# Work beside moved ahead of the second maximum, a reciprocal moved behind it, and one sequence's tokens turned in the first layers

## The chip, the core and the metric

The kernel runs on one core of a Trainium2 chip. Its engines each run their own queue in order: TensorE (PE in the profile; PEld is its loading of weights), VectorE (DVE), ScalarE (ACT), GpSimd (POOL) and SyncE (SP, which here only starts transfers). They wait for each other by semaphores. The metric is the device time of one execution in microseconds.

## The reference, cut to what is computed

Two sequences of 2048 tokens with 256 channels go through four layers, each with a layer norm in front and a residual around it.

```python
x = x + ssm(layernorm(x))         # state scan over the tokens, gelu, layer norm, nan_to_num
x = x + mixer(layernorm(x))       # sigmoid(xr Wr) * (relu(xk Wk)^2 Wv), xr and xk mix a token with the one before
x = x + attention(layernorm(x))   # 16 heads of 64, keys and values from a latent of 128, causal softmax
x = x + mixer(layernorm(x))
```

## The kernel before, in words

**Memory and banks.** X holds all tokens, 32 tiles of 128. There are 8 banks for products: 0 to 3 are `scores`, 4 `heads_out`, 5 and 6 `two_heads`, 7 `beside`.

**Order.** The class `Plan` writes one list of tasks, and each engine's program walks through that list and issues its part of each task. So the order of tasks is the order on every engine, and an engine whose part of a task waits holds up all of its parts of later tasks. `add` appends a task; `need` appends it with what it depends on, unless it is done.

**First layers** (`first_layers`, rounds k = 0 to 11). In round k the scan runs on block k (512 tokens), the tail of the first layer on block k-1, the first mixer's `turn`, `mix_tokens`, `products` and `square` on block k-2, and its `update` on block k-3. Blocks 0 to 3 are sequence 0. Behind round 7 the statistics of sequence 0 for the attention are complete (`inverse_std seq 0`, version 2). From round 8 on less and less work is left.

**Attention** (`attention`). All engines but SyncE's later part first wait until the last `update` is done (`attention_start`). For each pair of tiles `att_normal` (ScalarE, two normalisations `att_xn`), `turn_tiles` (TensorE transposes, a copy `att_xT_hi` on ScalarE, the rest `att_xT_lo` on VectorE) and for each block `latent` make the inputs. A unit is one sequence, one pair of heads and one block of 512 queries (j = 0 to 3); four units are a cycle, and there are 16 cycles. For a unit: `query`, `key` and `value` products; `maximum` (L755: two heads' scores into `two_heads`, and VectorE's reduction into `part_max`, L985, or L982 where the mask applies), whose next matmuls need the reduction before; `turn_max`; then steps over 128 keys each: `score` (L778 to L784), exponentials on ScalarE (L1194), sums on GpSimd (L1276), and `weigh` (L796, `heads_out`). At the end `denominators`, `invert` (the reciprocal L1010 and two small transfers by SyncE), `scale_out`, `two_parts` and `project`.

**The loop of steps** takes two steps at a time: a maximum of a later unit; the two scores; a second maximum; a filler; the two `weigh` of the pair before; a third maximum; other work. A filler is the open task with the earliest due time among query, key, value, latent, turn_tiles, turn_max and project; all write bank 7. A pair of steps is called diagonal where the causal mask cuts it (`scores<-scores,limit` on VectorE, L995): the last two pairs of each unit. In the first of them the scores have 512 and 384 columns, in the second 256 and 128. `query`, `key` and `project` have a part on VectorE (`q_lo`, `k_lo`, the sum into X), `value` and `turn_max` have none.

```python
            if at < goal:
                maximum()
            due("invert")
            for step in steps[s:s + 2]:
                self.need("score", *step)
            if at < goal:
                maximum()
            else:
                chore()
            filler(10 ** 6)
```

Of the kernel before, what the change touches and what calls it, by code (L numbers as in the profile page):

```python
# [5 lines left out]
ALU = mybir.AluOpType  # L6
ACT = mybir.ActivationFunctionType
# [5 lines left out]
P = 128  # L13
# [19 lines left out]
NDEN, QUAD = 8, 32  # L33
DVE_OUT = 62
# [22 lines left out]
class Plan:  # L57
# [104 lines left out]
    def first_layers(self):  # L162
# [15 lines left out]
        for k in range(NBL + 4):  # L178
# [38 lines left out]
            if k - 4 == NBLK - 1:  # L217
                self.add("inverse_std", "seq", 0, 0, NT, 2)

# [101 lines left out]
    def attention(self):  # L321
        self.freed = [None] * 8
        self.add("attention_start")
        self.need("turn_tiles", 0, 0)
        self.add("latent_weights")
# [57 lines left out]
        for s in range(0, len(steps) + 2, 2):  # L383
# [16 lines left out]
            filler(10 ** 6)  # L400
# [30 lines left out]
def build(nc, u, wA, wF, wKD, wPair, aDiag, h0, gb, mu, out):  # L431
# [4 lines left out]
    with ExitStack() as ctx:  # L436
# [26 lines left out]
        def empty(task, i=0):  # L463
# [11 lines left out]
        minus_mean_ok, zeros_ok, soft_v, soft_a, decay_ok = (  # L475
            sem(s) for s in ("minus_mean_ok", "zeros_ok", "soft_v", "soft_a", "decay_ok"))
# [25 lines left out]
        def channel_memory(where, w):  # L502
            return {"xn": sb(where, f"xnF{w}", [P, 2, TPB, C]), "xT": sb(where, f"xTF{w}", [P, 2, CH, BLK + 1]),
                    "mix": sb(where, f"mix{w}", [P, 2, 2, CH, BLK]), "relu": sb(where, f"relu{w}", [P, CH, BLK]),
                    "kact": sb(where, f"kact{w}", [P, 2, CH, BLK]),
                    "gate": sb(where, f"gate{w}", [P, 2, TPB, C])}

        M = {}
        with ExitStack() as tail_scope:
            gamma_beta = sb(tail_scope, "gamma_beta", [P, 2, C])  # L510
            G = sb(tail_scope, "G", [P, NB * NT, C])
            nrm = sb(tail_scope, "nrm", [P, 2, 2, C])
            clp = sb(tail_scope, "clp", [P, 2, 2, C])
            msk = sb(tail_scope, "msk", [P, 2, 2, C])
# [7 lines left out]
            zeros = sb(tail_scope, "zeros", [P, BLK])  # L522
            decay = sb(tail_scope, "decay", [P, CH, BLK])
# [5 lines left out]
        with ExitStack() as ph:  # L529
            axT_hi = sb(ph, "att_xT_hi", [P, CH, T], F32R)  # L530
            axT_lo = sb(ph, "att_xT_lo", [P, CH, T], F32R)
            lat_hi = sb(ph, "lat_hi", [P, T], F32R)
            lat_lo = sb(ph, "lat_lo", [P, T], F32R)
            axn = [sb(ph, f"att_xn{i}", [P, C]) for i in range(4)]
# [3 lines left out]
            wP_raw = sb(ph, "wP_raw", [P, WPC])  # L538
            kd_hi = sb(ph, "kd_hi", [P, CH, RANK], F32R)
            kd_lo = sb(ph, "kd_lo", [P, CH, RANK], F32R)  # L540
# [9 lines left out]
            kd_raw = prob[NPROB - 1][:, 0, 0:CH * RANK].rearrange("p (c r) -> p c r", c=CH)  # L550
# [831 lines left out]
```

## Time and profile before

| | |
|---|---|
| median of 3 runs | 2247.73 us (2247.59 to 2248.44) |
| profiled execution: its time, its span | 2246.04 us, 2244.7 us |
| TensorE busy | 2060.4 us (92%) |
| VectorE, ScalarE, GpSimd busy | 1331.9, 1102.8, 1426.5 us |
| TensorE busy in 0 to 56 us | 28.31 us, granted clock 0.97 |
| in 56 to 112, 112 to 168, 168 to 224 us | 51.08, 52.70, 47.56 us, clock 0.94, 0.97, 0.94 |
| in 224 to 280, 280 to 336 us | 35.07, 36.39 us, clock 0.76, 0.63 |
| in 800 to 900, 900 to 1000 us | 96.69, 96.07 us, clock 1.00, 0.98 |

### The profile page before, as it was taken

The page shows a single profiled execution, that of the slowest core. Times are in us where ns is not written, and L with a number is a line of the kernel's source. Part 1 is how long each engine was busy: PE and PEld are TensorE (multiplying, and loading weights), DVE is VectorE, ACT ScalarE, POOL GpSimd, SP SyncE. Part 2 cuts the span into 40 slices and gives each one's busy share as a digit, 9 for nine tenths or more (in the row PEclk, how much of TensorE's full clock was granted, in tenths as well). Part 3 has the DMA queues.
Part 4 walks back from the last instruction along what each step waited for, and adds up shares of the span by engine and source line. Part 5 has one row for each costly group of instructions (what it writes and reads, how often), then busy time and mean ns, then how long its engine had stood idle before and what let it go on. Part 6 is the DMA issues. An engine that isn't in the chain of part 4 may idle for free.

```text
span 2244.7 us, 35674 instructions
## 1 busy us (share of the span) xinstructions
PE 2060.4 (92%) x13104; PEld 1269.9 (57%) x13104; DVE 1331.9 (59%) x2713; ACT 1102.8 (49%) x2226; POOL 1426.5 (64%) x812
## 2 busy tenths in 40 slices
PE   5998669999999999999989999999999999999989
PEld 3666345555555555555555555555555555555556
DVE  5888446575656565656565656566656565656353
ACT  4775534444444444444454444444444444444575
POOL 0333305776777777777757677777777777777832
PEclk9999769999999999999999999999999999999999
DMA  3000000000000000000000000000000000000001
GB/s 108 1 1 1 10 7 6 10 18 10 18 11 18 11 18 11 18 11 18 10 18 11 13 11 19 9 22 6 19 9 23 11 18 11 18 11 11 25 24 57
DMA packets 25788, 37.03 MB, mean 16 GB/s; under 512 B 6544, under 2 KB 14864, under 8 KB 25616
## 3 DMA queue, kind: packets, MB, share of 16 engines
q1 hardware_dynamic: 25616, 34.76, 5.0%
q8 instruction: 106, 1.74, 0.3%
q14 instruction: 66, 0.54, 0.1%
HBM read 30.02 MB, written 4.46 MB: 15 GB/s over the span
## 4 chain that ended last, share of the span: by engine, by line
PE 65%; DVE 19%; ACT 6%; issue 5%; POOL 4%; DMA 0%; ACTq 0%; DVEq 0%; POOLq 0%
PE heads_out L796 18%; PE beside L615 14%; PE two_heads L755 8%; PE scores L778 4%; PE scores L784 4%; PE scores L782 4%; PE scores L780 4%; DVE part_max L985 4%; PE scores L615 2%; POOL acc L1276 2%; ACT prob L1194 2%; DVE stats L835 2%; PE beside L807 2%; PE beside L763 1%; PE two_heads L615 1%
## 5 line engine op out<-in xcount | busy, mean ns | idle before, releaser
L1276 POOL TENSOR_TENSOR acc<-acc,prob 128x1024 f32<-128x1024 f32 (+3 forms) x512 | 1017.1, 1987 | 228.5 <-ACT prob L1194 172.7
L1194 ACT ACTIVATE prob<-scores 128x512 f32<-128x512 f32 (+3 forms) x1280 | 579.4, 538 | 636.4 <-DVE scores L995 327.8
L985 DVE TENSOR_REDUCE part_max<-two_heads 128x2 f32<-128x1024 f32 x384 | 468.7, 1221 | 309.1 <-PE two_heads L755 308.8
L796 PE MATMUL heads_out<-prob,V 128*64 128x512 f32 (+3 forms) x2560 | 549.1, 550 | 0.0
L755 PE MATMUL two_heads<-k_hi,q_hi 64*128 64x512 f32 (+3 forms) x1280 | 278.9, 431 | 70.2 <-DVE part_max L982 36.5
L982 DVE CUSTOM_DVE_ANT_0 two_heads<-two_heads,mask 128x128 f32<-128x128 f32 (+3 forms) x512 | 241.8, 514 | 119.2 <-PE two_heads L755 119.1
L796 PEld LDWEIGHTS heads_out<-prob,V 128*64 128x64 f32 x2560 | 157.8, 138 | 232.1 <-issue 210.4
L755 PEld LDWEIGHTS two_heads<-k_hi,q_hi 64*128 64x128 f32 x1280 | 121.3, 186 | 239.3 <-issue 102.4
L778 PE MATMUL scores<-q_hi,k_hi 64*128 64x512 f32 (+3 forms) x1280 | 236.9, 364 | 1.0 <-ACT neg_max L1181 0.8
L784 PE MATMUL scores<-neg_max,sel 64*128 64x512 f32 (+3 forms) x1280 | 236.9, 363 | 0.0
L782 PE MATMUL scores<-q_lo,k_hi 64*128 64x512 f32 (+3 forms) x1280 | 236.3, 363 | 0.0
L780 PE MATMUL scores<-q_hi,k_lo 64*128 64x512 f32 (+3 forms) x1280 | 235.7, 362 | 0.0
L1271 POOL TENSOR_TENSOR acc<-prob 128x768 f32<-128x768 f32 (+1 forms) x64 | 144.0, 2250 | 139.7 <-ACT prob L1194 139.3
L1285 POOL TENSOR_TENSOR oT_lo<-oT,oT_hi 128x512 fp32r<-128x512 f32 x62 | 79.3, 1279 | 177.6 <-ACT oT_hi L1211 177.6
L1029 DVE TENSOR_TENSOR X<-X,beside 128x512 f32<-128x512 f32 x126 | 86.0, 683 | 91.3 <-PE beside L615 90.9
L782 PEld LDWEIGHTS scores<-q_lo,k_hi 64*128 64x128 f32 x1280 | 122.5, 185 | 19.0
L784 PEld LDWEIGHTS scores<-neg_max,sel 64*128 64x128 f32 x1280 | 122.6, 185 | 18.4
L780 PEld LDWEIGHTS scores<-q_hi,k_lo 64*128 64x128 f32 x1280 | 122.4, 186 | 18.7
L778 PEld LDWEIGHTS scores<-q_hi,k_hi 64*128 64x128 f32 x1280 | 122.4, 186 | 16.7 <-issue 5.0
L995 DVE TENSOR_TENSOR scores<-scores,limit 128x256 f32<-128x256 f32 x256 | 103.0, 430 | 21.5 <-PE scores L784 21.2
L968 DVE SCALAR_TENSOR_TENSOR q_lo<-beside,q_hi 128x512 fp32r<-128x512 f32 x62 | 42.9, 692 | 97.2 <-ACT q_hi L1163 97.2
L615 PE MATMUL beside<-wP_hi,oT_hi 128*128 128x256 f32 x252 | 84.6, 336 | 13.2 <-DVE X L1029 7.5
(298 smaller groups left out, 3011.4 us busy)
## 6 DMA issues: line engine op xcount, KB each, us to landing
rden<-rden_rows SPq DMA_DIRECT2D x128, 128.0 KB, 2.9
wP_raw<-wPair SPq DMA_DIRECT2D x16, 384.0 KB, 3.2
X<-u SPq DMA_DIRECT2D x8, 512.0 KB, 8.7
out<-X SPq DMA_DIRECT2D x8, 512.0 KB, 2.9
den<-den_rows SPq DMA_DIRECT2D x64, 4.0 KB
rden_rows<-inverse SPq DMA_DIRECT2D x64, 4.0 KB, 1.4
wA_sb<-wA SPq DMA_DIRECT2D x1, 768.0 KB, 6.8
wFa<-wF SPq DMA_DIRECT2D x1, 768.0 KB, 7.7
```

Source lines behind the costliest of these rows:

```text
L615: made = pe.matmul(dst, l, r, start=first and n == 0, stop=last and n == len(pairs) - 1)
L755: made = pe.matmul(two_heads[:, h, 0:width], q[head(h), t * P:(t + 1) * P], k[head(h), 0:width], start=True, stop=True)
L778: pe.matmul(bank(task, h)[:, x0:], k_hi[g][head(h), kc], q_hi[i][head(h), x0:], start=True, stop=False)
L780: pe.matmul(bank(task, h)[:, x0:], k_lo[g][head(h), kc], q_hi[i][head(h), x0:], start=False, stop=False)
L782: pe.matmul(bank(task, h)[:, x0:], k_hi[g][head(h), kc], q_lo[i][head(h), x0:], start=False, stop=False)
L784: pe.matmul(bank(task, h)[:, x0:], sel[head(h), :], neg_max[i][head(h), x0:], start=False, stop=True).then_inc(full(task, h)[0], 1)
L796: made = pe.matmul(heads_out[head(h), x0:], V[(idx - j + c) % NVS][:, tt, head(h)], prob[step % NPROB][:, h, x0:], start=t == 0, stop=t == ...
L982: made = ve.tensor_tensor_reduce(out=two_heads[:, h, 0:width], in0=two_heads[:, h, 0:width], in1=mask[:, BLK - width:], scale=1.0, scalar= ...
L985: made = ve.reduce_max(part_max[:, t, :, c:c + 1], two_heads[:, :, 0:width], AX.X)
L1194: ac.activation(prob[step % NPROB][:, h, x0:], bank(task, h)[:, x0:], ACT.Exp).then_inc(empty(task, h)[0], 1)
L1271: po.tensor_tensor(total[:, :, x0:], old[:, :, x0:], new[:, :, x0:], ALU.add).then_inc(acc_ok, 1)
L1276: po.tensor_tensor(total[:, :, x0:], total[:, :, x0:], new[:, :, x0:], ALU.add).then_inc(acc_ok, 1)
```

## The change

It has three parts. In the loop of steps, a pair that has a diagonal step takes its filler ahead of the second maximum, and `invert` is issued behind that maximum in every pair. In the first layers, the split of the latent's weights, all eight `turn_tiles` and the four `latent` of sequence 0 are issued in rounds 8, 9 and 10 (with NBL = 8), ahead of `attention_start`. The third part makes room: the tiles of the attention that are now written early get memory of their own (a scope `early` that closes behind the attention), and the first layers use less. `G` is a ring of three blocks, `msk` one buffer, `relu` is written into `kact` and squared in place, and the scan's factor `decay` is one column that is read repeated, for which `zeros` and the filling of `decay` go. The weights of the first pair of heads are loaded as soon as the latent's weights are split.

```diff
@@ first_layers
             if k - 4 == NBLK - 1:
                 self.add("inverse_std", "seq", 0, 0, NT, 2)
+                self.add("latent_weights")
+                self.need("att_normal", 0, 0)
+            if k == NBL:
+                for t in range(0, NT // 2, 2):
+                    self.need("turn_tiles", 0, t)
+            if k == NBL + 1:
+                for t in range(NT // 2, NT, 2):
+                    self.need("turn_tiles", 0, t)
+                self.need("latent", 0, 0)
+                self.need("latent", 0, 1)
+            if k == NBL + 2:
+                self.need("latent", 0, 2)
+                self.need("latent", 0, 3)
@@ attention
-        self.freed = [None] * 8
         self.add("attention_start")
-        self.need("turn_tiles", 0, 0)
-        self.add("latent_weights")
@@
         for n in range(TPB):
             maximum()
-            if n == 0:
-                self.need("turn_tiles", 0, TPB)
-            if n == 1:
-                self.need("latent", 0, 1)
@@
             if at < goal:
                 maximum()
-            due("invert")
             for step in steps[s:s + 2]:
                 self.need("score", *step)
+            diagonal = any(t >= TPB * UNITS[idx][2] for idx, t in steps[s:s + 2])
+            if diagonal:
+                filler(10 ** 6)
             if at < goal:
                 maximum()
             else:
                 chore()
-            filler(10 ** 6)
+            due("invert")
+            if not diagonal:
+                filler(10 ** 6)
@@ vector_program, ssm_setup and ssm_states
-                    ve.memset(zeros[:, :], 0.0).then_inc(zeros_ok, 1)
-                    for h in range(CH):
-                        ve.tensor_scalar(decay[:, h, :], zeros[:, :], a_col[:, h:h + 1], None, ALU.subtract).then_inc(decay_ok, 1)
+                    ve.tensor_scalar(decay[:, :], a_col[:, :], -1.0, None, ALU.mult).then_inc(decay_ok, 1)
-                        ve.tensor_tensor_scan(xs[:, s_, m, :], decay[:, m, :], bank(task, m), init, ALU.mult, ALU.add).then_inc(empty(task, m)[0], 1)
+                        ve.tensor_tensor_scan(xs[:, s_, m, :], decay[:, m:m + 1].broadcast_to([P, BLK]), bank(task, m), init, ALU.mult, ALU.add).then_inc(empty(task, m)[0], 1)
@@ scalar_program, ssm_output and products
+                        g = k % (NG * TPB)
+                        if i >= NG:
+                            w.wait_ge(normalised, plan.normal["tail_norm", k - NG * TPB] + 2)
-                        ac.activation(M[f]["relu"][:, m, :], bank(task, m), ACT.Relu).then_inc(empty(task, m)[0], 1)
+                        ac.activation(M[f]["kact"][:, i % 2, m, :], bank(task, m), ACT.Relu).then_inc(empty(task, m)[0], 1)
@@ sync_program
+            sp.dma_start(kd_raw[:, :, :], wKD).then_inc(kd_in, 16)
-                if kind == "attention_start":
-                    w.wait_ge(ffn["a"]["x_plus_ffn"], 2 * NBL)
-                    sp.dma_start(kd_raw[:, :, :], wKD).then_inc(kd_in, 16)
+                if kind == "latent_weights":
+                    w.wait_ge(kd_ok, 1)
                     sp.dma_start(wP_raw[:, :], wPair[0]).then_inc(wP_in, 16)
```

The order of instructions on VectorE at the first diagonal pair of a block 0, before (the `ISA` rows with 128x256 are the reduction of the second maximum, those with 128x384 that of the third):

```order
L995 TENSOR_TENSOR scores<-scores,limit 128x2x128 x2
L982 ISA two_heads,part_max<-two_heads,mask 128x256
L982 ISA part_max 128x1
L982 ISA two_heads,part_max<-two_heads,mask 128x256
L982 ISA part_max 128x1
L968 SCALAR_TENSOR_TENSOR q_lo<-beside,q_hi 128x512
L982 ISA two_heads,part_max<-two_heads,mask 128x384
```

and with the change:

```order
L1004 TENSOR_TENSOR scores<-scores,limit 128x2x128 x2
L977 SCALAR_TENSOR_TENSOR q_lo<-beside,q_hi 128x512
L991 ISA two_heads,part_max<-two_heads,mask 128x256
L991 ISA part_max 128x1
L991 ISA two_heads,part_max<-two_heads,mask 128x256
L991 ISA part_max 128x1
L991 ISA two_heads,part_max<-two_heads,mask 128x384
```

`q_lo` moved from behind the second maximum's reduction to ahead of it; on TensorE the six matmuls of `query` moved ahead of that maximum's.

VectorE again, in a pair of steps of block 1 that isn't diagonal, before (the reciprocal is `invert`, the two `wP_lo` a split of weights):

```order
L950 TENSOR_TENSOR wP_lo<-wP_raw,wP_hi 128x256
L1010 RECIPROCAL inverse<-den 16x64
L985 TENSOR_REDUCE part_max<-two_heads 128x2
L950 TENSOR_TENSOR wP_lo<-wP_raw,wP_hi 128x256
L973 TENSOR_TENSOR k_lo<-beside,k_hi 128x512
```

and with the change:

```order
L959 TENSOR_TENSOR wP_lo<-wP_raw,wP_hi 128x256
L994 TENSOR_REDUCE part_max<-two_heads 128x2
L959 TENSOR_TENSOR wP_lo<-wP_raw,wP_hi 128x256
L1019 RECIPROCAL inverse<-den 16x64
L982 TENSOR_TENSOR k_lo<-beside,k_hi 128x512
```

The reciprocal moved past the reduction and the second split, to just ahead of `k_lo`.

ScalarE in the first layers, behind round 8 (the square root `std` ends that round's statistics, `xnFa` is the normalisation of the last block for the mixer), before:

```order
L1119 ACTIVATE kacta<-relua 128x512 x2
L1042 ACT_TABLE_LOAD
L1042 ACTIVATE std<-std 128x4
L1035 ACTIVATE xnFa<-X,minus_mean,rstd 128x256 x4
L1090 ACTIVATE xTFa<-scores 128x512 x2
```

and with the change:

```order
L1130 ACTIVATE kacta<-kacta 128x512 x2
L1051 ACT_TABLE_LOAD
L1051 ACTIVATE std<-std 128x4
L1161 ACTIVATE att_xT_hi<-scores 128x2x256
L1044 ACTIVATE att_xn<-X,minus_mean,rstd 128x256 x2
L1161 ACTIVATE att_xT_hi<-scores 128x2x256
L1044 ACTIVATE att_xn<-X,minus_mean,rstd 128x256 x2
L1161 ACTIVATE att_xT_hi<-beside 128x2x256
L1044 ACTIVATE att_xn<-X,minus_mean,rstd 128x256 x2
L1161 ACTIVATE att_xT_hi<-scores 128x2x256
L1044 ACTIVATE att_xn<-X,minus_mean,rstd 128x256 x2
L1044 ACTIVATE xnFa<-X,minus_mean,rstd 128x256 x4
```

Four copies and four pairs of normalisations of the attention now stand ahead of the last block's normalisation. On TensorE the transposes between them stand ahead of the update of block 6.

## Rows read from the trace of the kernel before

**Rows 1.** The page's busy times: engine, us, share of the span, instructions

```profile
PE 2060.4 (92%) x13104; PEld 1269.9 (57%) x13104; DVE 1331.9 (59%) x2713; ACT 1102.8 (49%) x2226; POOL 1426.5 (64%) x812
```

**Rows 2.** TensorE's waits, 400 to 2110 us: us in total, times, longest

```profile
PE two_heads L755 <- DVE part_max L982: 30.6, 37, 1.8
```

**Rows 3.** Timeline, second diagonal pair of a block 2: start, us, instruction, idle before

```profile
965.62 0.69 DVE L973 TENSOR_TENSOR k_lo<-beside,k_hi 128x512 fp32r<-128x512 f32 x1 [3.10 <-ACT k_hi L1169]
...
967.42 0.50 PE L755 MATMUL two_heads<-k_hi,q_hi 64*128 64x512 f32 x2 [1.21 <-DVE part_max L982]
...
969.33 3.16 PE L796 MATMUL heads_out<-prob,V 128*64 128x512 f32 x8
```

**Rows 4.** Timeline of TensorE: the same place in other cycles

```profile
634.31 0.49 PE L755 MATMUL two_heads<-k_hi,q_hi 64*128 64x512 f32 x2 [1.21 <-DVE part_max L982]
...
747.48 0.50 PE L755 MATMUL two_heads<-k_hi,q_hi 64*128 64x512 f32 x2 [1.21 <-DVE part_max L982]
...
857.45 0.50 PE L755 MATMUL two_heads<-k_hi,q_hi 64*128 64x512 f32 x2 [1.21 <-DVE part_max L982]
...
1079.02 0.50 PE L755 MATMUL two_heads<-k_hi,q_hi 64*128 64x512 f32 x2 [1.21 <-DVE part_max L982]
...
1990.90 0.49 PE L755 MATMUL two_heads<-k_hi,q_hi 64*128 64x512 f32 x2 [1.21 <-DVE part_max L982]
```

**Rows 5.** Stretch: us, PE, PEld, DVE, ACT, POOL busy, granted clock, DMA share, GB/s

```profile
969.30:971.00 1.70, 1.70 (x6) 0.45 (x7) 0.24 (x3) 1.11 (x2) 0.37 (x1) 0.55 0.05 10
```

**Rows 6.** Timeline at the first diagonal pair of a block 0

```profile
907.37 1.85 ACT L1194 ACTIVATE prob<-scores 128x512 f32<-128x512 f32 x4 [2.68 <-DVE scores L995]
...
907.80 0.42 DVE L982 CUSTOM_DVE_ANT_0 two_heads<-two_heads,mask 128x256 f32<-128x256 f32 x1
...
908.52 0.14 DVE L982 DVE_READ_ACCUMULATOR2_ANT part_max<- 128x1 f32 x1
...
909.74 0.69 DVE L968 SCALAR_TENSOR_TENSOR q_lo<-beside,q_hi 128x512 fp32r<-128x512 f32 x1 [1.08 <-ACT q_hi L1163]
909.75 0.44 PE L755 MATMUL two_heads<-k_hi,q_hi 64*128 64x384 f32 x2
...
910.35 0.56 DVE L982 CUSTOM_DVE_ANT_0 two_heads<-two_heads,mask 128x384 f32<-128x384 f32 x1
...
911.53 0.51 PE L755 MATMUL two_heads<-k_hi,q_hi 64*128 64x512 f32 x2 [0.48 <-DVE part_max L982]
```

**Rows 7.** Timeline around a reciprocal in a pair that isn't diagonal

```profile
920.54 0.53 DVE L1010 RECIPROCAL inverse<-den 16x64 f32<-16x64 f32 x1
...
921.00 1.15 DVE L985 TENSOR_REDUCE part_max<-two_heads 128x2 f32<-128x1024 f32 x1
...
923.43 0.68 DVE L973 TENSOR_TENSOR k_lo<-beside,k_hi 128x512 fp32r<-128x512 f32 x1
...
924.16 0.64 PE L807 MATMUL beside<-acc,ones 128*32 128x256 f32 x8 [0.69 <-DVE k_lo L973]
```

**Rows 8.** Timeline of the start and of the hand-over to the attention

```profile
15.33 0.88 DVE L882 TENSOR_SCALAR decay<-zeros,a_col 128x512 f32<-128x512 f32 x2
...
271.68 1.09 ACT L1035 ACTIVATE att_xn<-X,minus_mean,rstd 128x256 f32<-128x256 f32 x2 [5.88 <-POOL X L1240]
...
273.83 0.60 ACT L1150 ACTIVATE att_xT_hi<-scores 128x512 fp32r<-128x512 f32 x1 [1.06 <-PE scores L702]
...
276.60 0.60 ACT L1150 ACTIVATE att_xT_hi<-scores 128x512 fp32r<-128x512 f32 x1 [1.20 <-PE scores L702]
...
283.00 0.80 PE L615 MATMUL scores<-lat_hi,wP_hi 128*128 128x512 f32 x1 [2.08 <-DVE wP_lo L950]
...
305.02 0.42 PE L778 MATMUL scores<-q_hi,k_hi 64*128 64x512 f32 x2
...
331.10 0.45 PE L778 MATMUL scores<-q_hi,k_hi 64*128 64x256 f32 x2
```

**Rows 9.** Chain of waits: the first latent (start, us, what)

```profile
278.02 2.91 PE beside L615 x6
```

More of the change, by code:

```diff
@@ L503, in channel_memory @@
             return {"xn": sb(where, f"xnF{w}", [P, 2, TPB, C]), "xT": sb(where, f"xTF{w}", [P, 2, CH, BLK + 1]),
-                    "mix": sb(where, f"mix{w}", [P, 2, 2, CH, BLK]), "relu": sb(where, f"relu{w}", [P, CH, BLK]),
-                    "kact": sb(where, f"kact{w}", [P, 2, CH, BLK]),
+                    "mix": sb(where, f"mix{w}", [P, 2, 2, CH, BLK]), "kact": sb(where, f"kact{w}", [P, 2, CH, BLK]),
                     "gate": sb(where, f"gate{w}", [P, 2, TPB, C])}
         M = {}
+        early = ctx.enter_context(ExitStack())
+        axT_hi = sb(early, "att_xT_hi", [P, CH, T], F32R)
+        axT_lo = sb(early, "att_xT_lo", [P, CH, T], F32R)
+        lat_hi = sb(early, "lat_hi", [P, T], F32R)
+        lat_lo = sb(early, "lat_lo", [P, T], F32R)
+        axn = [sb(early, f"att_xn{i}", [P, C]) for i in range(4)]
+        kd_hi = sb(early, "kd_hi", [P, CH, RANK], F32R)
+        kd_lo = sb(early, "kd_lo", [P, CH, RANK], F32R)
+        wP_raw = sb(early, "wP_raw", [P, WPC])
+        kd_raw = wP_raw[:, 0:CH * RANK].rearrange("p (c r) -> p c r", c=CH)
         with ExitStack() as tail_scope:
             gamma_beta = sb(tail_scope, "gamma_beta", [P, 2, C])
-            G = sb(tail_scope, "G", [P, NB * NT, C])
+            G = sb(tail_scope, "G", [P, NG * TPB, C])
             nrm = sb(tail_scope, "nrm", [P, 2, 2, C])
             clp = sb(tail_scope, "clp", [P, 2, 2, C])
-            msk = sb(tail_scope, "msk", [P, 2, 2, C])
+            msk = sb(tail_scope, "msk", [P, 2, C])
             fin = sb(tail_scope, "fin", [P, 2, 2, C], mybir.dt.uint32)
@@ L521, in build @@
             a_col = sb(tail_scope, "a_col", [P, CH])
-            zeros = sb(tail_scope, "zeros", [P, BLK])
-            decay = sb(tail_scope, "decay", [P, CH, BLK])
+            decay = sb(tail_scope, "decay", [P, CH])
             state0 = sb(tail_scope, "state0", [P, CH])
@@ L561, in build @@
             oT_lo = sb(ph, "oT_lo", [P, BLK], F32R)
+        early.close()
         with ExitStack() as ph:
@@ L1114, in scalar_program @@
                     _, f, i = task
-                    if i >= 2:
-                        w.wait_ge(*full(("update", f, i - 2), 1))
                     for m in range(CH):
                         w.wait_ge(*empty(("products", f, i), m))
-                        ac.activation(M[f]["kact"][:, i % 2, m, :], M[f]["relu"][:, m, :], ACT.Square).then_inc(ffn[f]["kact"], 1)
+                        ac.activation(M[f]["kact"][:, i % 2, m, :], M[f]["kact"][:, i % 2, m, :], ACT.Square).then_inc(ffn[f]["kact"], 1)
                 elif kind == "attention_start":
```

30 lines of the change are left out of this document (11 added, 19 removed).

## Prediction, written before the changed kernel was run

> **What bounds the kernel now.** I read the busy row of the page first. TensorE is busy for 2060.4 of 2244.7 us, 92%, and every other engine 64% or less [rows 1]. So TensorE's idle time is what a change of order can win or lose, about 184 us. The stretches in the table ahead put 85 us of it before 336 us, in the first layers and the start of the attention; in the long middle TensorE is 96 to 97% busy. There the list of waits shows one wait that matters to this change: the `two_heads` matmuls of a maximum wait for VectorE to have read the maximum before, 30.6 us in 37 waits on L982 alone [rows 2]. Then I read three places of one cycle (four units of one pair of heads, about 110 us, sixteen of them) in the order of time, and last the hand-over from the first layers to the attention.
>
> **Part 1: the filler ahead of the second maximum, where it wins.** In the diagonal pairs the filler now stands before the maximum. It can only fill a wait where there is a filler, and where TensorE waits. Both hold at the second diagonal pair of block 2, where the filler is `value`: TensorE waits 1.21 us there, and starts the four `heads_out` products behind the value product at 969.33 [rows 3]. This wait stands in nearly every cycle, thirteen times between 519 and 1991 us (twice 1.76 us), of which six stand here [rows 3, 4]. With `value` in front, TensorE can start it when bank 7 is free, that is when `k_lo` ends at 966.31 (965.62 + 0.69), instead of sitting until 967.42. The value product lasts 1.48 us whichever way, so about 1.0 us of the 1.21 is won and 0.3 us of waiting for the bank is left. VectorE has nothing to do for `value`, so nothing gets in front of the second reduction. 14 places x 1.0 = **-14 us**. The waits in the other second pairs, like the 0.48 us at 911.53 [rows 6], have no filler behind them and stay.
>
> **The clock there.** Behind the wait at 967.42 the granted clock is 0.55 in the next 1.70 us [rows 5], near the lower of the two levels (1.2 GHz). Five of the thirteen places are followed by such a stretch. The price is in the distance between equal places: 109.97 us from 747.48 to 857.45 and the same on to 967.42, but 111.60 from 967.42 to 1079.02 and 113.17 from 634.31 to 747.48 [rows 3, 4]. So a drop costs 1.6 us, or 3.2 where it lasts longer; all five together some 11 us. If the wait is gone, I expect them gone.
>
> **Part 2: where it loses.** At the first diagonal pair of block 0 the filler is `query`, and `query` has a part on VectorE, `q_lo`, which now stands ahead of the second maximum's reduction. `q_lo` cannot be early: it waits for `q_hi` on ScalarE, which comes behind the four exponentials of 907.37 (1.85 us), whatever TensorE does. So it starts at 909.74 as now [rows 6]. The reduction of the second maximum, which ran in 907.80 to 908.66 and so 0.86 us, then starts where the next one starts now, 910.35, and ends at 911.21. TensorE follows 0.05 us behind such an end (911.48 to 911.53), so the next maximum starts at 911.26 instead of 909.75: a **new wait of 1.5 us**. Behind it on TensorE are the next score pair and everything else; its cover is only the short `heads_out` products of the block that ends (256 and 128 columns, 0.8 us). The wait at 911.53 comes 1.78 us behind 909.75 and moves along, so nothing is won back. 15 places x 1.5 = **+22.5 us**. The fillers `project`, `turn_max` and `value` in the other first pairs are free: there 1.7 us of `heads_out` products stand between the second maximum and the next, more than a reduction of 1.2 us, and no wait is there now to fill.
>
> **Part 3: the reciprocal behind the second maximum.** It takes 0.53 us on VectorE and now often runs while VectorE would wait. Ahead of `k_lo` at 923.43 the chain on VectorE is full: the reduction at 921.00 began 0.4 us late because of the reciprocal at 920.54. Moved behind, it lets the reduction start at about 920.75 and holds `k_lo` up by 0.3 us; TensorE waits for that `k_lo` already, 0.69 us at 924.16 [rows 7]. In two more places of a cycle it lands in front of a bank's reading for which TensorE comes almost at once, some 0.15 us each. That is 0.6 us x 15 = **+9 us**, between 0 (the chain has slack) and 0.8 x 16 = 13. The transfers that it starts come 2 to 3 us later; GpSimd would wait for them about as long once a cycle, and is idle for longer than that before its next reading of ScalarE's copy. I cost it at nothing; if the slack is not there, up to 1 us a cycle.
>
> **Part 4: sequence 0's tokens in the first layers.** The cost first. A pair of tiles (two normalisations, four transposes, a copy, a subtraction) is a closed circle of ScalarE and TensorE: 2.77 us from copy to copy (273.83 to 276.60) [rows 8]. In the last-but-one round four such pairs now stand on ScalarE ahead of the last block's normalisation: three circles and the rest of one, 9.9 us, on the path. One normalisation more (1.09 us) stands ahead in the round before. In the last round three circles stand between the squares and the last block's update on TensorE, 8.2 us, and two latents, 2.91 us each at the lower clock [rows 9]. Sum: 24.9 us, which moves the first key product from 283.00 to about 298, because the 11.3 us from 271.68 to it fall to about 1.6 us (only the weights' split is left). That is +15. Now the gain. From key to first score, 22.0 us now (283.00 to 305.02), two pairs and a latent go: about -5. From there to the second score pair, 26.1 us (to 331.10), two pairs, a latent and the wait behind it go: -7.4. The last two pairs and latent, and their waits, go from the next 30 us: -3. So this is about level when the clock stays as low as now (0.63 in 280 to 336 us, by the table ahead), and -9 us if TensorE, busier before the last products, gets its full clock back sooner. I take **-3**, with -10 and +7 as ends.
>
> **Small terms.** `decay` and `zeros` leave the start: the two operations of 0.88 us at 15.33 stand right before the statistics on which all waits [rows 8]; **-0.7**. The scan reads its factor as one column repeated; no row shows that form, and I take the same 1.26 us, 0.3 us more or less for each of sixteen. `relu` into `kact`, one `msk`, the ring `G`: each new wait is for something done long before.
>
> **Sum.** Waits: -14 + 22.5 + 9 - 3 - 0.7 = +13.8. Clock: the five drops go (-11), but the new place is idle for 1.5 and then 0.48 us within 3.3 us, more than at the old one. I let half of the fifteen drop at 1.6 us, +12, and set both to nothing. The profiled execution took 2246.04 us, 1.7 us under the median of 2247.73; its time with the sum is 2259.8, and counted from the median, as a run would be compared, it is 2261.5: I forecast **2261 us**.
>
> On the clock the Trainium skill (TensorE: Matmul & The Clock Gate, A second HAM failure mode: psum-queue depth-cycling) tells of a kernel whose TensorE idles briefly between groups of matmuls often enough for the clock to go back and forth, so that throughput suffers more than by the idle time. By that, the new place should drop in most cycles; the trace has it in five of thirteen at the old one.
>
> **Rivals.** (a) *The clock gains and nothing is paid for it*: the drops at `value` go, `query` brings none. For it: eight of the thirteen waits at `value` brought none. 2261 - 12 = 2249 us, no change. (b) *Faster*: the same, and TensorE also holds its full clock from the last update on, so that part 4 gives its -9 or -10. It decides whether the last block's products of 512 columns, now at half rate for their first 4 us, run at full rate. 2249 - 7 = 2242, and 2238 if half of part 3 is slack. (c) *The clock falls at `query` in nearly every cycle*, some of them for the longer 3.2 us: 13 x 1.6 to 2 more than nothing, less the half I counted: 2261 + 12 = 2273, up to 2282. (d) *The change doesn't do it*: the order shows `q_lo` ahead of the reduction in fifteen places and `value` ahead in thirteen, so this is out.
>
> **Chances.** Forecast (2252 to 2266) 0.42; (c) and worse 0.20; (a) 0.23; (b) 0.15. A measurement of this kernel can tell about 0.2% (4.5 us) from no change. Slower by more than that 0.60, within it 0.25, faster 0.15. The range 2242 to 2282 leaves out the far ends of (b) and (c).
>
> **What would show it.** In the profile after: a wait of about 1.5 us of `two_heads` for `part_max` behind each `q_lo` of block 0, with `q_lo` ahead of a 256-column reduction; no wait over 0.4 us before `value`; 0.9 to 1.0 us instead of 0.69 before the denominators; the cycle longer by 1 us where no drop falls; first key product at 293 to 300 us and second score pair at 325 to 335. Wrong it would be if the wait at `query` is under 0.5 us, or if the attention's first step starts past 320 us.

## The result, and the profile after

The changed kernel takes 2251.64 us in the median of ten runs, the kernel before 2246.31 us in ten runs beside them: a ratio of 1.0027, with a 95% interval of 1.0017 to 1.0036. It is slower by some 5 to 6 us, the way that was forecast, and inside the range; but the forecast said +14, more than twice as much. The profiled execution has a span of 2249.3 us, 4.6 more than before (2244.7).

The busy row of the page, and the waits of TensorE in 400 to 2110 us (us in total, times, longest), of the changed kernel:

```profile
PE 2058.6 (92%) x13104; PEld 1263.7 (56%) x13104; DVE 1344.5 (60%) x2711; ACT 1100.2 (49%) x2226; POOL 1424.4 (63%) x812
...
PE two_heads L767 <- DVE part_max L991: 26.1, 34, 1.3
PE two_heads L767 <- DVE part_max L994: 19.9, 37, 1.6
PE beside L819 <- DVE k_lo L982: 15.3, 14, 1.1
...
PE beside L627 <- DVE k_lo L982: 2.9, 14, 0.6
```

Against [rows 2], the masked maxima (now L991) cost 26.1 us and not 30.6: much of one wait went and much of another came. The denominators' wait for `k_lo` went from 10.0 to 15.3 us in fourteen places. The last row is what is left at `value`.

**One cycle without a clock drop.** The denominators' product stands once in every unit and serves as a mark. Four stretches between five marks make a cycle. The timeline rows of these marks (start, duration, instruction, the wait before it), first of before, then of after:

```profile
803.66 0.64 PE L807 MATMUL beside<-acc,ones 128*32 128x256 f32 x8
814.20 0.64 PE L807 MATMUL beside<-acc,ones 128*32 128x256 f32 x8 [0.69 <-DVE k_lo L973]
835.18 0.64 PE L807 MATMUL beside<-acc,ones 128*32 128x256 f32 x8
872.40 0.64 PE L807 MATMUL beside<-acc,ones 128*32 128x256 f32 x8
913.62 0.64 PE L807 MATMUL beside<-acc,ones 128*32 128x256 f32 x8
```

```profile
796.15 0.64 PE L819 MATMUL beside<-acc,ones 128*32 128x256 f32 x8
807.09 0.64 PE L819 MATMUL beside<-acc,ones 128*32 128x256 f32 x8 [1.10 <-DVE k_lo L982]
828.11 0.64 PE L819 MATMUL beside<-acc,ones 128*32 128x256 f32 x8
864.36 0.64 PE L819 MATMUL beside<-acc,ones 128*32 128x256 f32 x8
907.16 0.64 PE L819 MATMUL beside<-acc,ones 128*32 128x256 f32 x8
```

The four differences are 10.54, 20.98, 37.22 and 41.22 us before, and 10.94, 21.02, 36.25 and 42.80 after. I call the stretches K (the wait for `k_lo` is in it), N, V (the place of `value` in block 2) and Q (the place of `query`). K is longer by 0.40, N by 0.04, V shorter by 0.97, Q longer by 1.58: +1.05 us a cycle.

**The place of `query`.** TensorE and VectorE of the changed kernel, where [rows 6] stood before:

```profile
901.30 0.87 PE L808 MATMUL heads_out<-prob,V 128*64 128x256 f32 x8
901.86 0.69 DVE L977 SCALAR_TENSOR_TENSOR q_lo<-beside,q_hi 128x512 fp32r<-128x512 f32 x1 [1.83 <-ACT q_hi L1174]
902.47 0.42 DVE L991 CUSTOM_DVE_ANT_0 two_heads<-two_heads,mask 128x256 f32<-128x256 f32 x1
...
903.19 0.14 DVE L991 DVE_READ_ACCUMULATOR2_ANT part_max<- 128x1 f32 x1
903.39 0.44 PE L767 MATMUL two_heads<-k_hi,q_hi 64*128 64x384 f32 x2 [1.22 <-DVE part_max L991]
...
905.07 0.51 PE L767 MATMUL two_heads<-k_hi,q_hi 64*128 64x512 f32 x2 [0.37 <-DVE part_max L991]
```

VectorE waits 1.83 us for ScalarE before `q_lo`, reduces the 256-column maximum only behind it, and the next maximum's matmuls wait 1.22 us. The wait after that one is 0.37 instead of 0.48 us.

**The place of `value`**, where the 1.21 us of [rows 3] stood. A wait of 0.18 us is left, and the maximum behind the product has none:

```profile
960.40 0.33 PE L627 MATMUL beside<-wP_hi,lat_hi 128*128 128x128 f32 x1 [0.18 <-DVE k_lo L982]
...
961.89 0.50 PE L767 MATMUL two_heads<-k_hi,q_hi 64*128 64x512 f32 x2
```

**The hand-over**, where [rows 8] gave 283.00, 305.02 and 331.10: first key product, first score, second score pair.

```profile
294.94 0.47 PE L627 MATMUL beside<-lat_hi,wP_hi 128*128 128x512 f32 x1 [2.17 <-DVE wP_lo L959]
...
311.23 0.42 PE L790 MATMUL scores<-q_hi,k_hi 64*128 64x512 f32 x2
...
329.43 0.41 PE L790 MATMUL scores<-q_hi,k_hi 64*128 64x256 f32 x2
```

The first denominators' product starts at 349.81 us and not at 353.39: 3.6 us earlier.

**The clock.** A stretch-by-stretch view with slices of 3 us (PE, PEld, DVE, ACT, POOL busy, granted clock, DMA share, GB/s) around a `query` place at which the clock fell, behind the waits of 1.22 and 0.37 us at 1709.79 and 1711.47:

```profile
1707.00:1710.00 3.00, 1.78 (x14) 0.89 (x15) 1.47 (x5) 1.83 (x4) 2.13 (x2) 1.00 0.00 0
1710.00:1713.00 3.00, 2.63 (x24) 1.64 (x24) 2.73 (x9) 1.00 (x4) 0.41 (x2) 0.81 0.00 0
1713.00:1716.00 3.00, 3.00 (x18) 0.76 (x16) 0.59 (x3) 0.14 (x1) 1.60 (x2) 0.62 0.00 0
```

What the lower level takes, the loss, is (1 - granted clock) times 3 us, summed over such slices: here 0.57 + 1.14 = 1.7 us. Between 336 and 2110 us every drop in every trace of this study comes to 1.7 us or twice that, except where 2110 us cuts one. In sum it is 17.0 us before (five drops at `value` places, 11.9 us, and three others, one of them behind a wait for ScalarE's `att_xn` between the two sequences) and 12.0 us after (five at `query` places, 8.5 us, and two others; none at `value`).

So a span splits in two: this loss, and the rest. Before it is 2227.7 + 17.0, after 2237.3 + 12.0: **+9.6 us of rest, and 5.0 us that the clock gives back.** The rest isn't all at full clock. In 0 to 336 us, where TensorE is often idle, the same sum is 44.4 us before and 39.2 after. A cleaner measure of the waits in the loop is the time from the first to the 63rd of the marks less the loss in it: 1740.4 us before and 1753.5 after, **+13.1 us**. The first mark is 3.6 us earlier, and that makes the +9.6 within 0.1 us. The experiments ask which part does what, and whether the parts add up.

### The profile page after: what moved, and what is told of

Read it like the earlier page. It is cut to its first block, busy times and chain, and to the rows that moved or that the text cites. A ratio compares the mean times of both kernels' runs of the same rounds, so it can differ in the third digit from the quotient of the medians.

```text
span 2249.3 us, 35656 instructions
## 1 busy us (share of the span) xinstructions
PE 2058.6 (92%) x13104; PEld 1263.7 (56%) x13104; DVE 1344.5 (60%) x2711; ACT 1100.2 (49%) x2226; POOL 1424.4 (63%) x812
## 4 chain that ended last, share of the span: by engine, by line
PE 69%; DVE 17%; ACT 7%; issue 5%; POOL 2%; DMA 0%; ACTq 0%; DVEq 0%; SPq 0%; POOLq 0%
PE heads_out L808 19%; PE beside L627 14%; PE two_heads L767 9%; PE scores L790 5%; PE scores L796 5%; PE scores L794 5%; PE scores L792 4%; PE scores L627 3%; DVE part_max L994 3%; ACT prob L1205 2%; PE beside L819 2%; DVE stats L847 2%; DVE X L1038 2%; PE beside L775 1%; DVE two_heads L991 1%
## 5 line engine op out<-in xcount | busy, mean ns | idle before, releaser
L991 DVE CUSTOM_DVE_ANT_0 two_heads<-two_heads,mask 128x128 f32<-128x128 f32 (+3 forms) x512 | 242.0, 514 | 147.3 <-PE two_heads L767 147.1
L1292 POOL TENSOR_TENSOR oT<-oT,rden 128x512 f32<-128x512 f32 x62 | 79.2, 1278 | 128.3 <-DMA rden<-rden_rows 106.1
L790 PEld LDWEIGHTS scores<-q_hi,k_hi 64*128 64x128 f32 x1280 | 121.8, 186 | 15.8 <-issue 4.0
```

The source lines that it names most:

```text
L790: pe.matmul(bank(task, h)[:, x0:], k_hi[g][head(h), kc], q_hi[i][head(h), x0:], start=True, stop=False)
L991: made = ve.tensor_tensor_reduce(out=two_heads[:, h, 0:width], in0=two_heads[:, h, 0:width], in1=mask[:, BLK - width:], scale=1.0, scalar= ...
```

## The experiments

The table has the medians of all kernels, the ratio to the kernel before with its 95% interval, the profile's span split as above, and the four stretches of a cycle without a drop. Each kernel is compared with the kernel before as timed beside it.

| kernel | median us | ratio to before (95%) | span = rest + loss in 336 to 2110 us | K, N, V, Q |
|---|---|---|---|---|
| before | 2246.3 to 2247.8 | 1 | 2244.7 = 2227.7 + 17.0 | 10.54, 20.98, 37.22, 41.22 |
| changed | 2251.64 | 1.0027 (1.0017 to 1.0036) | 2249.3 = 2237.3 + 12.0 | 10.94, 21.02, 36.25, 42.80 |
| a1_invert_alone | 2255.22 | 1.0032 (1.0020 to 1.0045) | 2254.6 = 2232.4 + 22.2 | 10.94, 20.83, 37.3, 41.2 |
| a2_query_alone | 2287.37 | 1.0186 (1.0159 to 1.0212) | 2291.9 = 2247.5 + 44.4 | 10.53, 20.96, 37.3, 42.6 |
| a3_others_alone | 2223.95 | 0.9899 (0.9883 to 0.9916) | 2222.7 = 2217.6 + 5.1 | 10.53, 21.15, 36.2, 41.4 |
| a4_front_alone | 2245.34 | 1.0001 (0.9987 to 1.0016) | 2246.5 = 2222.6 + 23.9 | 10.53, 20.97, 37.3, 41.2 |
| b1_q_lo_behind | 2231.80 | 0.9932 (0.9920 to 0.9945) | 2231.6 = 2223.0 + 8.6 | 10.94, 21.02, 36.2, 41.76 |
| b2_all_but_query | 2219.49 | 0.9877 (0.9862 to 0.9892) | 2220.3 = 2213.5 + 6.8 | 10.53, 21.17, 36.2, 41.4 |
| b3_value_ahead | 2221.30 | 0.9892 (0.9875 to 0.9909) | 2218.1 = 2207.3 + 10.8 | 10.53, 20.96, 36.2, 41.2 |
| b5_value_invert_last | 2231.56 | 0.9932 (0.9919 to 0.9944) | 2228.9 = 2217.0 + 11.9 | 10.53, 20.84 then 21.8, 36.2, 41.2 |
| c1_value_alone | 2220.59 | 0.9892 (0.9871 to 0.9912) | 2219.8 = 2211.3 + 8.5 | 10.53, 20.95, 36.2, 41.2 |
| c2_value_and_query | 2244.52 | 1.0014 (0.9996 to 1.0032) | 2242.9 = 2229.2 + 13.7 | 10.54, 20.95, 36.2, 42.6 |
| c3_front_again | 2247.62 | 1.0024 (1.0004 to 1.0044) | 2254.5 = 2223.8 + 30.7 | 10.54, 20.94, 37.3, 41.2 |
| c4_value_held | 2206.33 | 0.9835 (0.9809 to 0.9861) | 2205.6 = 2197.1 + 8.5 | 10.53, 20.28, 36.2, 41.2 |

The second table keeps the start apart from the loop, and looks at more than one execution. Every execution has its granted clock on record, to three digits; (1 - granted clock) x span is its loss over the whole length. The last two columns are means over all executions of a kernel, good to about 1 us (the kernel before has a rest of 2180.1 and a loss of 65.0 us, to which the changed kernel is compared; the others are compared with the executions beside them).

| kernel | first mark, us | marks 1 to 63 less their loss, against before | all executions: rest, against before | loss, against before |
|---|---|---|---|---|
| before | 353.39 | 0 | 0 | 0 |
| changed | 349.81 | +13.1 | +15.8 | -10.5 |
| a1_invert_alone | 352.99 | +3.4 | +3.3 | +4.1 |
| a2_query_alone | 353.05 | +18.4 | +19.4 | +23.1 |
| a3_others_alone | 354.35 | -9.4 | -7.0 | -15.6 |
| a4_front_alone | 348.85 | -0.4 | -1.2 | +1.2 |
| b1_q_lo_behind | 348.12 | -2.2 | -0.3 | -15.0 |
| b2_all_but_query | 346.98 | -10.6 | -11.6 | -15.5 |
| b3_value_ahead | 349.45 | -14.3 | -13.4 | -11.0 |
| b5_value_invert_last | 347.97 | -6.3 | -5.2 | -10.1 |
| c1_value_alone | 351.37 | -14.3 | -13.2 | -12.0 |
| c2_value_and_query | 348.98 | +6.0 | +7.9 | -5.1 |
| c3_front_again | 350.86 | -1.5 | +0.5 | +5.1 |
| c4_value_held | 350.25 | -24.1 | -23.3 | -14.7 |

The rows before, a1, a2, c1 and c2 have moved nothing ahead of the first mark, and still it comes between 348.98 and 353.39 us. So a start that is some us earlier in one trace says little.

### The reciprocal alone (a1_invert_alone)

```diff
             if at < goal:
                 maximum()
-            due("invert")
             for step in steps[s:s + 2]:
                 self.need("score", *step)
             if at < goal:
                 maximum()
             else:
                 chore()
+            due("invert")
             filler(10 ** 6)
```

> The kernel before with one part of the change alone: the reciprocal stands behind the second maximum, in all pairs. The waits' theory, from the trace of the changed kernel: the denominators' wait for k_lo grows from 0.69 to 1.10 us, and the next stretch by 0.04, once a cycle, so +0.44 x 15 = +6.6 us, about 1.003 of before. The rival, that the reciprocal costs nothing and the two maxima before k_lo are late because of the other edits: within 1 us of before, and the wait stays at 0.69.

The wait for `k_lo` of this kernel (waits of TensorE, 400 to 2110 us):

```profile
PE beside L807 <- DVE k_lo L973: 15.6, 14, 1.4
```

K grows from 10.54 to 10.94, as expected; but N falls from 20.98 to 20.83, so a cycle costs 0.25 to 0.28 us. Between the marks that is 3.4 us, half of what was expected. The medians say 7.6 us; the rest is clock, 5.2 us more loss in this trace and 4.1 in the mean of its executions.

### The query alone (a2_query_alone), and the clock that its shift costs elsewhere

```diff
+            if diagonal and coming() == "query":
+                filler(10 ** 6)
+                diagonal = None
             if at < goal:
                 maximum()
             else:
                 chore()
-            filler(10 ** 6)
+            if diagonal is not None:
+                filler(10 ** 6)
```

(`coming()` gives the kind of the filler that would be taken; `diagonal` is as in the change.)

> The kernel before with the filler ahead of the second maximum of a diagonal pair only where the filler is query (fifteen places). The waits' theory: each such stretch of a cycle is longer by 1.2 us of waits and 0.2 to 0.4 us of the changed order on TensorE, together 1.4 to 1.6, so +21 to +24 us. The clock theory adds to this: the new place is followed by a stretch at the lower clock in some seven cycles, 1.6 us or more each, while the five drops at value stay, so +33 to +39 us (1.015 to 1.017). The rival, that the clock falls about equally often whatever the order is: +21 to +24 us (1.010).

It lost 40 us, just above the 33 to 39 us of the upper theory. The waits of TensorE in 400 to 2140 us, and the two slices around the `value` place at 862.33, where the wait was 1.22 us, as before:

```profile
PE two_heads L764 <- DVE part_max L991: 46.7, 52, 1.8
...
861.00:864.00 3.00, 1.78 (x12) 1.43 (x11) 3.00 (x10) 1.00 (x4) 1.08 (x1) 0.88 0.00 0
864.00:867.00 3.00, 3.00 (x12) 1.65 (x13) 0.44 (x3) 1.11 (x2) 0.66 (x1) 0.50 0.00 0
```

Between the marks, without the loss, it costs 18.4 us, Q being longer by 1.4. Some 27 us of this trace are clock (23 in the mean of its six executions), and they do not lie at `query` alone, where the clock fell in seven of fifteen places: at the untouched `value` places the clock fell in ten of thirteen cycles, where it had fallen in five, and often for twice as long (V of 40.4 us instead of 37.3 or 38.9).

### The other fillers alone (a3_others_alone)

The same edit with `coming() != "query"`.

> The kernel before with the filler ahead only where it is value, turn_max or project; query and the reciprocal stay where they were. The waits' theory: -0.96 us at each of thirteen places of value in block 2, nothing or up to +0.2 us at each of the 43 others (a change of the matmuls' form on TensorE that costs a little), so -12 to -5 us. With the clock theory, the drops that follow the wait at value go too, another -11 to -15 us: -16 to -27 us (0.988 to 0.993). The rival, that the clock falls about equally often whatever the order: -5 to -12 us (0.995 to 0.998).

24 us faster than before, as the clock theory had it. V is 36.2 us in all the regular cycles. But Q and N are longer by 0.17 each: `project`, `turn_max` and `value` of block 1, ahead where TensorE had nothing to wait for, cost that.

### Sequence 0 in the first layers alone (a4_front_alone, c3_front_again)

The changed kernel with the loop's lines as they were before. The second kernel is the first again, the same program.

> The changed kernel with the loop of the kernel before: only the tokens of sequence 0 in the first layers and the changed memory are left. From the trace of the changed kernel: the first denominators' product starts at 349.81 instead of 353.39 us, so -3.6 us, and nothing after it: -3 to -4.5 us (0.998 to 0.9987). The rival, that the buffers' new places or the other parity of the banks cost something in the loop, so that what the whole change lost beyond the waits comes from here: 0 to +6 us.

> The changed kernel with the loop of before once more, to narrow its interval: sequence 0's tokens in the first layers, and the memory, alone. If the 4.5 us by which the loop starts earlier come through: 0.998 to 0.999 of before. If the clock drops that its trace showed at the first block, between the sequences and at the end (1.4, 3.4 and 1.4 us more than before) come in most runs, they take it back: 0.9995 to 1.001.

The first mark comes at 348.85 and 350.86 us, in the mean 2.3 us earlier than in the five kernels with the old first layers named above, whose own spread is larger. In the times nothing arrives: the medians are 2.3 below and 0.6 above before, and the ratio of c3_front_again, 1.0024, lies above both ranges that were expected. Nor is there a clear gain without the clock: over all executions the rest is 1.2 us below and 0.5 above before.

The lower clock was moved about. The last stretch of the hand-over, first of before, then of the changed kernel (a4 and c3 too have less loss there):

```profile
309.00:336.00 27.00, 15.75 (x57) 9.49 (x57) 12.88 (x28) 6.27 (x14) 4.16 (x4) 0.56 0.00 0
```

```profile
309.00:336.00 27.00, 17.49 (x85) 10.62 (x84) 16.18 (x32) 7.10 (x15) 4.14 (x4) 0.75 0.05 15
```

The loss is 12.0 us before and 6.8 after. Behind it, the slices of a4_front_alone at the first units, and the same of before:

```profile
342.00:345.00 3.00, 3.00 (x16) 2.36 (x16) 1.55 (x2) 0.88 (x2) 0.00 (x0) 0.50 0.00 0
...
360.00:363.00 3.00, 3.00 (x12) 1.00 (x10) 1.09 (x1) 1.30 (x5) 1.99 (x2) 0.58 0.03 7
```

```profile
342.00:345.00 3.00, 2.60 (x22) 1.43 (x18) 1.94 (x3) 2.82 (x6) 1.10 (x1) 1.00 0.00 0
...
360.00:363.00 3.00, 2.40 (x23) 1.68 (x21) 2.79 (x7) 0.60 (x1) 1.79 (x1) 1.00 0.00 0
```

Two drops stand there that before does not have, 3.4 us, and both traces show them. The two traces of this one program have spans of 2246.5 and 2254.5 us, 8 us apart, of which 6.8 are loss at the lower clock: so far did the clock alone move one execution.

### The q_lo put back behind the reduction (b1_q_lo_behind)

The changed kernel, edited in VectorE's program alone:

```diff
+            behind = list(tasks)
+            for n in range(1, len(behind) - 1):
+                if [behind[n + i][0] for i in (-1, 0, 1)] == ["score", "query", "maximum"]:
+                    behind[n], behind[n + 1] = behind[n + 1], behind[n]
-            for task in tasks:
+            for task in behind:
```

> The changed kernel with one thing undone: on VectorE alone q_lo stands behind the second maximum's reduction again, at the sixteen places where query stands ahead of the second maximum; TensorE and ScalarE keep the changed order. The theory that q_lo ahead of the reduction makes the new wait: the wait of 1.22 us goes to 0, the stretch of a cycle with it falls from 42.79 to about 41.4 us, and with it the seven drops of the clock behind it, so 15 x 1.3 = 20 us and some 10 to 15 us of clock below the changed kernel: 2216 to 2232 us. The rival, that TensorE's own order (the maximum's products behind those of query) makes the wait: it stays over 0.8 us and the time within 5 us of 2252.

```profile
896.77 0.45 PE L767 MATMUL two_heads<-k_hi,q_hi 64*128 64x384 f32 x2 [0.17 <-DVE part_max L995]
898.45 0.50 PE L767 MATMUL two_heads<-k_hi,q_hi 64*128 64x512 f32 x2 [0.37 <-DVE part_max L995]
```

The wait is 0.17 us instead of 1.22 with TensorE's order unchanged, Q falls from 42.80 to 41.76, no drop stands at `query` any more, and the kernel is 20 us faster than the changed one, at the slow end of what was expected (a wait of 0 and a Q of 41.4 us). So `q_lo` ahead of the reduction made the wait. That is shown. What is left of `query` ahead, Q of 41.76 against 41.40 in b2_all_but_query, is the price of TensorE's own order: the wait of 0.17 us and 0.2 us without a wait.

### Leaving query behind, and which fillers pay (b2_all_but_query, b3_value_ahead)

> The changed kernel with query behind the second maximum and the reciprocal where it was before; value, turn_max and project stay ahead, and the first layers as in the change. If the parts add up: 2224 from the kernel with the others ahead, less 0 to 3 us for the first layers, 2220 to 2225 us (0.988 to 0.990 of before). If the first layers' part is worth nothing at all or a loss, as the time of that part alone leaves open: 2224 to 2228 us.

> As the kernel with all but query ahead, but only value in the second diagonal pair of block 2 is ahead (thirteen places); value of block 1, turn_max and project stand behind as before. The theory that the change of the matmuls' form costs about 0.2 us at each of the 43 places where no wait is there to fill: two stretches of each cycle go back from 41.39 to 41.22 and from 21.15 to 20.96 us, 0.36 x 15 = 5 us less than with all but query, 2214 to 2220 us. The rival, that the order at these places is free and the difference in the two stretches comes from the other parts: within 2 us of it, 2219 to 2226 us.

In b3_value_ahead the filler goes ahead under `coming() == "value" and UNITS[steps[s][0]][2] == 2`. Both are some 27 us faster than before. Between the marks b3 is 3.7 us below b2, as the theory of the cost at the other places has it, if less than its 5 us (Q 41.4 to 41.2, N 21.17 to 20.96). In the medians b3 is 1.8 us slower, inside the rival's range; its loss is 4.5 us more in the mean of all executions. So the cost of 0.2 us in each of the two stretches is seen in the traces, and not in the times.

### The reciprocal behind the maxima (b5_value_invert_last)

`due("invert")` stands directly ahead of the `weigh` of the pair before; the rest is b3_value_ahead.

> As the kernel with value alone ahead, but the reciprocal stands behind the filler and the maxima of its pair, directly ahead of the next weigh, and so behind k_lo. The theory that VectorE's queue ahead of k_lo is full: without the reciprocal in it the denominators' wait falls from 0.69 to 0.3 to 0.45 us, 0.25 to 0.4 us a cycle, 4 to 6 us faster, 2209 to 2215 us. The rival, that the maxima before it wait for TensorE anyway, so that the wait stays at 0.69, and the later transfers hold up GpSimd: 0 to 8 us slower than with value alone.

10 us slower, the rival, and somewhat more than its 8. K stayed at 10.53 us, so the reciprocal had not been what held up `k_lo` before. And in the second sequence TensorE waits for GpSimd in each cycle (timeline, one of eight):

```profile
1721.67 0.36 PE L632 MATMUL beside<-wP_hi,oT_hi 128*128 128x256 f32 x1 [1.59 <-POOL oT_lo L1301]
```

A reciprocal that comes still later starts its two transfers later, GpSimd scales later, and the projection waits.

### Value alone, and value with query (c1_value_alone, c2_value_and_query)

> The kernel before with one thing changed: value ahead of the second maximum in the second diagonal pair of block 2 (thirteen places). Against the kernel with the same place and the changed first layers too (0.9892 of before, 2221 us): if the first layers are worth the 3.5 to 5 us by which the first denominators' product is earlier, this one takes 2224 to 2227 us (0.990 to 0.992); if they are worth nothing, 2219 to 2223. In the trace the stretch with value is 36.2 us in all the cycles and no clock drop stands in it.

> The kernel before with value of block 2 and query of block 0 ahead of the second maximum, nothing else. The theory that the two places share their clock drops (query alone made the stretch with value longer too, because the wait there then met a drop in ten cycles and not in five): with the wait at value filled, query costs only what its own stretch shows, 30 to 32 us less about 2.5 for the other fillers, so this kernel is 24 to 29 us above value alone, 2246 to 2254 us (1.000 to 1.003). The rival, that query costs 40 us wherever it stands ahead, as when it was moved alone: 2260 to 2266 us (1.006 to 1.009).

In c2 the filler goes ahead under `coming() in ("query", "value") and UNITS[steps[s][0]][2] in (0, 2)`.

c1, thirteen places of the kernel before reordered and nothing else, gives 26 of the 27 us: 14.3 in waits between the marks, the rest clock (12.0 in the mean of its executions; 8.5 in this trace, whose first mark is 2.0 us early as well). Its ratio equals that of b3 to the fourth digit, which again finds no time in the first layers' part. c2 lies 24 us above c1 (27 by the ratios), at the lower edge of the first theory and far from the 40 us of query alone. Query costs 20.3 us between the marks there; the loss grows by 5 us in the traces (7 over all executions) and not by 27. So the parts add up in waits and do not in clock: with the wait at `value` filled, the shift that `query` brings has no drops to multiply.

### Value of block 1 held back too (c4_value_held)

```diff
+            first = diagonal and steps[s][1] == TPB * UNITS[steps[s][0]][2]
+            held = first and coming() == "value" and UNITS[steps[s][0]][2] == 1
+            if diagonal and not held and coming() == "value" and UNITS[steps[s][0]][2] in (1, 2):
+                filler(10 ** 6)
+                diagonal = None
```

> As the kernel with value alone ahead and the changed first layers, but value of block 1 too is held back from the first diagonal pair to the second and stands there ahead of the second maximum, where TensorE waits 0.46 us for a reduction of 512 columns. If the wait is filled, less 0.2 us for the changed form of the matmuls: 0.2 to 0.4 us at thirteen places, 3 to 5 us faster, 2216 to 2219 us. The rival, that value's bank comes free only behind the wait or that the first pair without a filler opens a wait of its own: 0 to 5 us slower, 2221 to 2226 us.

The maximum in question, first in b3_value_ahead, then in c4_value_held:

```profile
811.37 0.50 PE L772 MATMUL two_heads<-k_hi,q_hi 64*128 64x512 f32 x2 [0.46 <-DVE part_max L999]
```

```profile
806.68 0.50 PE L774 MATMUL two_heads<-k_hi,q_hi 64*128 64x512 f32 x2
```

N falls from 20.96 to 20.28 us, 0.68 and not the 0.2 to 0.4 expected (why it is more than the wait of 0.46 was not taken apart), and the kernel takes 2206.33 us: 41 us less than before, and 45 less than the changed one. It beats both. The change takes `value` of block 1 in the first diagonal pair, where nothing waits; this kernel takes it one pair later, where TensorE waits.

## Why the prediction was right or wrong, point by point

**The places and mechanisms** held. The wait at `value` went, all but 0.18 us (0.3 was said); the wait at `query` came, with `q_lo` in front of a 256-column reduction; the denominators' wait went to 1.1 us (0.9 to 1.0 was said); the first key product came at 294.94 (293 to 300) and the second score pair at 329.43 (325 to 335); a cycle without a drop is 1.05 us longer (1 us). A scan with its factor as one repeated column took 1262 ns, as before.

**Term by term**, without the clock's loss, with the medians beside it:

| term | forecast us | traces without the loss, from | medians |
|---|---|---|---|
| value | -14 | -14.3 (c1) | -26.4, with its drops |
| query | +22.5 | +20.3 (c2 less c1), +18.4 (a2) | +23.9 (c2 less c1) |
| other fillers ahead | 0 | +4.9 (a3 less c1), +3.7 (b2 less b3) | +2.7 |
| reciprocal | +9 | +3.4 (a1) | +7.6 |
| first layers and small terms | -3.7 | -3.6 at the first mark of the change; in the mean of a4 and c3 -2.3 | -2.3, +0.6 |
| clock | 0 (-11, +12) | | in the rows above |
| sum | +13.8 | parts +7.6 to +10.7; the change itself +9.5 | parts +5.5 to +8.4; the change itself +5.3 |

**The steps that failed.** First, the sum of the clock. The forecast set -11 against +12 and took both as nothing; they left -5.0 us between 336 and 2110 us (-10.5 over the whole length, in the mean of ten executions). The -11 was near (11.9 us of drops at `value`, and one of 1.7 elsewhere, were gone), but the +12 for `query` was set from a guess that half of fifteen places would drop; five did, 8.5 us. The argument had been that a place with 1.5 and 0.48 us of idle time within 3.3 us is worse than the old one with 1.21. At `query` the sum of waits was 1.59 us, and the clock fell there about as often as at `value` before; where `query` alone was moved, it fell in seven. Second, Part 3. The wait for `k_lo` grew by 0.41 us, more than the 0.3 said, but the two further places of +0.15 us do not exist; instead stretch N got shorter by 0.15. 0.6 us a cycle was 0.28, and +9 was +3.4. Third, Part 2 took 1.5 us a place for a wait of 1.5 us. The wait was 1.22 and the next one 0.11 shorter; TensorE's own order, which was put at nothing, cost 0.2 more, and with it Q was 1.41 us longer.

Two terms came out partly by luck. Part 1 multiplied by 14 places where there are thirteen; the total held because two of them, with waits of 1.76 us, gave 1.44 us each (39.17 to 37.73 in V). And the start agrees with the forecast to 0.1 us, while kernels with the same order up to there differ by over 4 us.

**What was missed** has the other sign. Part 2 called `project`, `turn_max` and `value` of block 1 free because no wait was there to fill or to make. They cost 0.17 to 0.2 us in each of two stretches, 4 to 5 us between the marks. The rows at `query` show the same in small: from the last score's start to `heads_out` went 1.97 us before (906.98 to 908.95) and 2.18 after (899.12 to 901.30), with the same matmuls between in another order and no wait. TensorE now goes from matmuls of 64 rows to such of 128 twice there and not once. Whether it is the step between matmuls of 64 and of 128 rows that costs this was not tried alone.

**The rivals.** (a), no change with 2249 us, came closest in size and was right on the clock at `value`; it was wrong in that `query` did bring drops, and the waits cost less than the 13.8 us it counted on. (b) fell: the loop began 3.6 us earlier, but the medians of the first layers' part alone show no gain. (c) fell for the whole change. Query alone did cost 40 us, but not in (c)'s way: the clock fell at `query` in seven of fifteen places and not in nearly all, and most of the added loss lay at `value`.

**The page of the Trainium skill** (TensorE: Matmul & The Clock Gate, A second HAM failure mode: psum-queue depth-cycling) says of another kernel that brief idling between groups of matmuls makes the clock go back and forth and costs throughput. The traces agree in kind: the drops stand behind such waits, and none stands in the 117 `value` places of the nine kernels in which the wait was filled. They don't bear out the "most cycles" that the forecast drew from it: the same wait of 1.21 us was followed by a drop in five, seven, ten, five and seven of thirteen places, in before, a1, a2, a4 and c3.

What stays open is what decides in which cycles a wait of 1.2 us is followed by a drop. It changed with orders that did not touch the place (a2), and between two executions of one program (a4 and c3).

## What to carry to other kernels

Work beside is worth moving only to a place where the engine waits, and only such work as puts nothing in front of what it waits for on the other engine: `value` gave 26 us in thirteen places, `query` took 24 in fifteen, and a stretch without a wait paid 0.2 us for the move. Take one rule apart by kind of filler before judging it. And cost waits and clock in separate sums: the waits of the parts added up to within about 2 us, the clock did not, since a shift of the rhythm can change how often every other wait is followed by a drop. Where the wait at `value` was filled, its drops were gone in all nine orders.

## What the runs showed of the hardware that was not expected

Between 336 and 2110 us the lower clock came in portions: 1.7 or 3.4 us lost, in all fourteen traces, whatever the place. One reordering of fifteen places, costing 18 us in waits, raised this loss from 17.0 to 44.4 us. Two executions of one program differed by 6.8 us in it. And the wait for `k_lo` did not fall when VectorE had 0.53 us less to do ahead of it (b5, 0.70 us as before), though it rose by 0.41 when the same operation came between the second maximum and `k_lo` (a1): so there was slack ahead of that maximum and none behind it.
